# A pairwise embedding tower: chunk 7 of the second batch tile is gathered instead of looked up, under a batch schedule of its own

## The chip, the core and the metric

The kernel runs on one core of one Trainium2 chip. The metric is the device time of one execution, in microseconds (us); three runs of the kernel before have a median of 761.44 us (761.08 to 764.19). Engines are named as in the profile: PE is TensorE, DVE is VectorE, ACT is ScalarE, POOL is GpSimd, SP is the engine that issues most DMAs.

## The reference

2048 samples have 39 ids each. Every id picks a row of 32 numbers from its field's table. For all 741 pairs (i, j) of fields a bilinear form of the two rows is taken with a 32 x 32 matrix of that pair; the 741 sums and 16 dense numbers go through a network of three layers.

```python
e = stack([tbl_f[ids[:, f]] for f in range(39)], axis=1)        # 2048 x 39 x 32
p, q = e[:, ROW, :], e[:, COL, :]                                # all 741 pairs i < j
z = einsum('bpc,apc,bpa->bp', p, w, q)                           # w: 32 x 741 x 32
h = concatenate([z, dense_ctx], axis=1)                          # 757 wide
h = maximum(h @ W_top1 + b_top1, 0)                              # 512
h = maximum(h @ W_top2 + b_top2, 0)                              # 256
y = h @ W_top3                                                   # 1
```

All of it is float32. Products with the pair weights and with the looked-up rows are made of split parts (a rounded part and its rest), so nothing of a value is dropped.

## The kernel before

**Tiles, chunks, batches.** The 2048 samples are 4 tiles of 512. The 39 fields are 10 chunks of four fields (chunk 9 has three); a chunk is named (tile, chunk), as (1, 7). In each tile 200 units are worked through: one unit is one field j against one chunk of partners. Two units are a step, four are a batch. A tile has 50 batches; batches are counted through here, so that tile 1 is batches 50 to 99 and batch 54 is the fifth of tile 1.

**A batch.** PE multiplies four times pair weights by a chunk's stacked values (`u_ps`, line 590). DVE multiplies two units at a time by the partners' values (`prod`, line 911); this needs what PE wrote and releases PE's next but one step. PE sums the products of the batch before (`z_ps`, line 614). In tiles 1 to 3 the batch may hold a piece of the previous tile's network (`m_ps`, line 627, two matmuls of 128x512; called a piece). Where several units of a batch are summed in the same quarter of PE's columns, that sum takes longer.

**How a chunk gets its rows.** Either POOL gathers them: one indirect DMA for each field and each 128 samples, 16 for a chunk (line 419), which land in `e_rows`, and PE turns them around into `t_ps` (`turn`, line 525, four matmuls at line 534). Or, for chunks of small tables (`HOT_TABLES`), they are looked up: DVE compares the ids with row numbers (`one_hot`, line 899), and PE multiplies the result by the table, held in SBUF in three bf16 parts (`look_up`, line 540, matmuls at line 553). A chunk has 10 such slices; slices 0 to 7 have all four fields and 12 matmuls, the last two only the fields of larger tables. Chunks 1, 7 and 8 are looked up in every tile, chunk 2 in tile 0 alone. Three `one_hot` buffers are in turn (`OS = 3`).

After that ACT copies `t_ps` twice (lines 717 and 722), DVE makes the rest (`split_chunk`, line 865), SP stores both to DRAM (`store_parts`) and loads them back in another layout (`stack_chunk`, line 477) into one of four `e4` slots; the first unit of the chunk waits for that load. The first five chunks of tile 0 (`MADE`) are laid out by PE and ACT instead (`make_half`, `take_half`).

**What sets the order.** The tables `FIRST_TILE` and `OTHER_TILES` give, for each chunk: its number, whether it is of the next tile, the batch in which it is turned, and the batches in which its slices are looked up. In a batch PE does its units, a network piece if there is one, the sum of the batch before, then turns, then slices. DVE does two multiplies, then the split of a chunk that was completed in the batch before, then the one-hots of the next batch, then in tile 0 a part of the pair weights' rest (`weights_low`). `spread_mlp` puts the network's 34 pieces into batches with little else. Everything is in order on each engine, with semaphores between.

**Gathers.** POOL issues the gathers in the order of the chunks. The first 96, all of tile 0, wait for the landing of the gather three before (`WINDOW = 3`, line 416). From number 96 on (counted from 0) a gather waits only for a multiply: `s_mul` must reach 45 + (n - 96) * 100 // 108, so 108 gathers are spread over 100 steps (line 418). Number 96 is the first gather of (1, 2). A chunk's gathers also wait until the chunk four places before it has been turned.

Of the kernel before, what the change touches and what calls it, by code (L numbers as in the profile page):

```python
# [10 lines left out]
NT = B // NB  # L11
# [19 lines left out]

def hot(c):

    return c[1] in HOT_TABLES and (c[1] != 2 or c[0] == 0)


def gathered(c):
# [53 lines left out]
def place_sums():  # L91
# [4 lines left out]
    for g, gi, j in UNITS:  # L96
# [9 lines left out]
        if room > n:  # L106
# [12 lines left out]

PACED_FROM, PACE_LEAD = 96, 52  # L120
GATHERS_PER_TILE = 108

E4_SLOT = {0: 0, 1: 2, 2: 3, 3: 1, 7: 2, 8: 3, 4: 0, 5: 1, 6: 0, 9: 1}
OS = 3
# [7 lines left out]
PREPS_FIRST = 2  # L132
PREPS = {max(4 * k - 11, 2 * k - 3 if k < 4 else 6): k for k in range(PREPS_FIRST, len(PREP_UNITS))}

PREP_LOADS = {max(2 if k == 3 else 4, 4 * k - 15, k + 1 if k > 4 else 0): k for k in range(3, len(PREP_UNITS))}

BEGIN = (1, 0)
FIRST_TILE = ((2, 0, 0, (0, 0, 0, 1, 1, 1, 1, 1)), (7, 0, None, (1, 1, 1, 1, 1, 2, 2, 2, 2, 2)), (3, 0, 3, ()), (4, 0, 7, ()),  # L140
# [3 lines left out]
OTHER_TILES = ((8, 0, None, (0, 1, 1, 2, 3, 4, 4, 5, 6, 6)), (4, 0, 7, ()),  # L144
# [12 lines left out]


def chunks_of_tile(t):
    return [x for x in (OTHER_TILES if t else FIRST_TILE) if t + x[1] < NT]  # L160


ORDER = [(0, g) for g in BEGIN] + [(t + nxt, g) for t in range(NT) for g, nxt, turn, slices in chunks_of_tile(t)]
# [81 lines left out]
NI = len(ITEM)  # L245


def spread_mlp(last):

    work = {}  # L250
    for b in range(3, 39 if last else 48):
        slices = sum(list(x[3]).count(b) for x in OTHER_TILES if not (last and x[1]))
        work[b] = 3 * slices + (3 if any(x[2] == b for x in OTHER_TILES) else 0)
    taken = []
    for n in range(len(MLP)):
        b = min(work, key=lambda b: (work[b], b))
        work[b] += 4
        taken.append(b)
    return sorted(taken)


MLP_AT = {last: spread_mlp(last) for last in (False, True)}


def mlp_pieces(batch, last):
    return [piece for piece, b in zip(MLP, MLP_AT[last]) if b == batch]


def ends_tile(tile):
# [11 lines left out]
def tower(nc, tables, ids, hot_ids, hot_rows, dense, w, w1, b1, w2, b2, w3, sel_in, ident_in, y):  # L281
# [4 lines left out]
    with ExitStack() as ctx:  # L286
# [115 lines left out]
        @block.gpsimd  # L402
        def _(pool):
            pool.wait_ge(s_idx, 16)
            issued = 0
            for c in GATHERED:
                t, g = c
                r = GPOS[c] % ER
                if GPOS[c] >= ER:
                    pool.wait_ge(s_tp, GPOS[c] - ER + 1)  # L410
                for q in gathered(c):
                    f = C * g + q
                    for n in range(TPG):
                        if GPOS[c] > 1 and issued < PACED_FROM:
                            before = issued - WINDOW
                            pool.wait_ge(s_rows[GPOS[GATHERS[before]] % ER][before % WINDOW], landed(before))
                        if issued >= PACED_FROM:
                            pool.wait_ge(s_mul, PACED_FROM - PACE_LEAD + 1 + (issued - PACED_FROM) * NS // GATHERS_PER_TILE)
                        pool.indirect_dma_start(  # L419
                            e_rows[:, r, n, D * q:D * q + D], None, tables[f],  # L420
                            bass.IndirectOffsetOnAxis(ap=idx[:, t, f * TPG + n:f * TPG + n + 1], axis=0),
                        ).then_inc(s_rows[r][issued % WINDOW], 16)
                        issued += 1
# [92 lines left out]
        def _(pe):  # L516
# [162 lines left out]
            for t in range(NT):  # L679
                for b in range(NBAT):  # L680
                    for x in range(SPB):
                        interact(t, SPB * b + x)
                    if t:
                        for piece in mlp_pieces(b, t == NT - 1):
                            mlp_piece(t - 1, *piece)
                    if b:
                        reduce(t, b - 1)
                    elif t:
                        reduce(t - 1, NBAT - 1)
                    for c in TURNS.get(NBAT * t + b, ()):  # L690
                        turn(c)
                    for c, k in TAKES.get(NBAT * t + b, ()):
                        look_up(c, k)
                    if t == 0:
                        for c, half in MADE_IN.get(b, ()):
                            make_half(c, half)
                    if t == NT - 1:
                        for m, k in EARLY.get(b, ()):
                            early_piece(t, m, k)
# [3 lines left out]
        def _(act):  # L703
# [121 lines left out]
            for t in range(NT):  # L825
                for b in range(NBAT):
                    if t:
                        for layer, m, k in mlp_pieces(b, t == NT - 1):
                            if k == LAYER_INPUTS[layer] - 1:
                                take_mlp(t - 1, layer, m, m_ps[:, :])  # L830
                    for tile in range(NZ):
                        done = ends_tile(tile) // UPB + 1
                        if done == b:
                            take_z(t, tile)
                        elif t and done == NBAT and b == 0:
                            take_z(t - 1, tile)
                    for c in COMPLETE.get(NBAT * t + b, ()):
                        take_chunk(c)
                    if t == 0:
                        for c, half in MADE_IN.get(b, ()):  # L840
                            take_half(c, half)
                        if b == LAST_TABLE_BATCH:
                            table_high(HOT_CHUNKS[-1])
                        if b == LAST_TABLE_BATCH + 2:
                            table_middle(HOT_CHUNKS[-1])
                        if b - 1 in PREPS:
                            weights_rest(PREPS[b - 1])
                        if b in PREPS:
                            weights_high(PREPS[b])
                        if b in PREP_LOADS:  # L850
                            load_weights(PREP_LOADS[b])
# [7 lines left out]
        def _(dve):  # L859
# [81 lines left out]
            for t in range(NT):  # L941
                for b in range(NBAT):
# [7 lines left out]
                    if t == 0:  # L950
                        if b == LAST_TABLE_BATCH + 1:
                            table_rest(HOT_CHUNKS[-1])
                        if b == LAST_TABLE_BATCH + 3:
                            table_low(HOT_CHUNKS[-1])
                        for c in COMPLETE.get(b, ()):
                            if c in MADE:
                                split_chunk(c)
                    for c, k in TAKES.get(NBAT * t + b + 1, ()):
                        one_hot_slice(c, k)
                    if t == 0 and b in PREPS:  # L960
                        weights_low(PREPS[b])

# [58 lines left out]
```

## Time and profile before

| | |
|---|---|
| three runs, median (lowest to highest) | 761.44 us (761.08 to 764.19) |
| the profiled execution: its own time | 762.68 us |
| its span in the trace | 760.8 us |
| mean granted clock of PE, share of full speed | 0.978 |
| PE busy | 711.1 us (93%) |
| DVE busy | 610.1 us (80%) |
| POOL busy | 411.7 us (54%) |
| ACT busy | 104.5 us (14%) |
| first multiply of tiles 0, 1, 2 and 3 starts at | 40.21, 236.07, 403.67, 572.26 us |

The busy shares are means over stages with different limits. The last line says where the time goes: tile 0 takes 196 us from its first multiply, tiles 1 and 2 take 168 and 169, tile 3 and the end of the network the last 189.

### The profile page before, as it was taken

How to read it: one execution, taken by the hardware profiler on the slowest of the kernel's cores; microseconds unless marked ns; L12 is line 12 of the kernel's file. 1: busy time of each engine (PE TensorE's matmuls, PEld its weight loads, DVE VectorE, ACT ScalarE, POOL GpSimd, SP SyncE). 2: the span in 40 equal slices, each digit the busy share in tenths (PEclk: the TensorE clock that was granted, in tenths of full speed). 3: DMA queues.
4: the chain of work that ended last, by engine and by line, in shares of the span. 5: the costliest groups of instructions: out<-in, count | busy, mean ns of one | idle time of the engine just before them, and what ended most of it. 6: DMA issues, size and time to landing. Idle time of an engine off the chain costs nothing.

```text
span 760.8 us, 10920 instructions
## 1 busy us (share of the span) xinstructions
PE 711.1 (93%) x4202; PEld 285.7 (38%) x4202; DVE 610.1 (80%) x773; ACT 104.5 (14%) x186; POOL 411.7 (54%) x424
## 2 busy tenths in 40 slices
PE   0778888798999999999999999999999999999998
PEld 0233233333334444443434444444334434343343
DVE  3675798899989997998879987998879877788640
ACT  3413301111110100110110101011010101011002
POOL 5777546577776565667656555667655566000000
PEclk9787999999999999999999999999999999999999
DMA  7633987869868382739675472747656373553100
GB/s 205 192 115 87 321 314 235 312 217 307 288 212 289 112 264 75 243 72 307 179 243 184 143 259 64 234 117 243 226 185 233 100 253 88 167 174 105 69 0 0
DMA packets 72271, 141.40 MB, mean 186 GB/s; under 512 B 13829, under 2 KB 23704, under 8 KB 72092
## 3 DMA queue, kind: packets, MB, share of 16 engines
q1 hardware_dynamic: 48796, 116.86, 44.4%
q0 software_dynamic: 13440, 6.91, 6.6%
q10 hardware_dynamic: 9984, 16.94, 6.3%
q8 instruction: 33, 0.54, 0.3%
q14 instruction: 18, 0.15, 0.1%
HBM read 109.66 MB, written 31.00 MB: 185 GB/s over the span
## 4 chain that ended last, share of the span: by engine, by line
PE 81%; DVE 8%; issue 4%; DMA 3%; POOL 2%; ACT 1%; ACTq 0%; SPq 0%; DVEq 0%
PE z_ps L614 26%; PE u_ps L590 26%; PE t_ps L553 10%; PE m_ps L627 8%; DVE prod L911 5%; PE m_ps L629 3%; POOL e_rows L419 2%; DVE one_hot L899 2%; PE t_ps L534 2%; PE u_ps L649 1%; DMA e<-scratch 1%; PE u_ps L658 1%; PE m_ps L631 1%; PE t_ps L641 1%; PE m_ps L641 1%
## 5 line engine op out<-in xcount | busy, mean ns | idle before, releaser
L911 DVE TENSOR_TENSOR prod<-u_ps,eT 128x1024 f32<-128x1024 f32 x400 | 469.6, 1216 | 93.6 <-PE u_ps L590 92.7
L419 POOL DMA_INDIRECT e_rows<-in_tbl_dram,idx x420 | 411.5, 980 | 234.9 <-DVE prod L911 109.5
L590 PE MATMUL u_ps<-e,w 128*128 128x512 f32 x800 | 254.9, 433 | 17.8 <-DVE prod L911 12.9
L614 PE MATMUL z_ps<-prod,sel 128*32 128x512 f32 x1600 | 263.0, 613 | 0.0
L590 PEld LDWEIGHTS u_ps<-e,w 128*128 128x128 f32 x800 | 133.7, 190 | 159.8 <-DVE prod L911 75.8
L553 PE MATMUL t_ps<-one_hot,tb 125*32 125x512 bf16 x1344 | 134.1, 394 | 10.2 <-DVE one_hot L899 8.7
L899 DVE TENSOR_SCALAR one_hot<-hot_idx,row 125x512 bf16<-125x512 f16 (+2 forms) x296 | 108.2, 421 | 13.7 <-PE t_ps L553 11.9
L614 PEld LDWEIGHTS z_ps<-prod,sel 128*32 128x32 f32 x1600 | 43.6, 108 | 137.4 <-issue 111.1
L553 PEld LDWEIGHTS t_ps<-one_hot,tb 125*32 125x32 bf16 x1344 | 48.8, 98 | 91.5 <-issue 59.4
L627 PE MATMUL m_ps<-zT,w1s 128*128 128x512 f32 x144 | 73.5, 592 | 0.0
L717 ACT CAST parts<-t_ps 128x512 fp32r<-128x512 f32 (+1 forms) x40 | 23.5, 587 | 216.1 <-PE t_ps L553 125.1
L781 ACT COPY zT<-z_ps 128x512 f32<-128x512 f32 x24 | 14.1, 587 | 202.0 <-PE z_ps L614 202.0
L865 DVE TENSOR_TENSOR parts<-eT,parts 128x512 fp32r<-128x512 f32 (+1 forms) x40 | 27.2, 680 | 3.8 <-ACT eT L722 3.8
L627 PEld LDWEIGHTS m_ps<-zT,w1s 128*128 128x128 f32 x144 | 27.1, 188 | 6.3
L788 ACT ACTIVATE h<-m_ps,b1s 128x512 f32<-128x512 f32 x13 | 9.0, 689 | 138.4 <-PE m_ps L627 137.1
L629 PE MATMUL m_ps<-h,w2s 128*128 128x512 f32 x48 | 24.5, 592 | 0.0
L722 ACT COPY eT<-t_ps 128x512 f32<-128x512 f32 (+1 forms) x40 | 23.7, 591 | 0.0
L534 PEld LDWEIGHTS t_ps<-ident,e_rows 128*128 128x128 f32 (+2 forms) x112 | 12.2, 143 | 26.3 <-issue 22.9
L534 PE MATMUL t_ps<-ident,e_rows 128*128 128x128 f32 (+2 forms) x112 | 19.3, 298 | 2.6 <-DMA e_rows<-in_tbl_dram,idx 2.6
L872 DVE TENSOR_TENSOR h<-h 128x512 fp32r<-128x512 f32 (+1 forms) x13 | 8.6, 665 | 3.5 <-ACT h L748 3.5
L748 ACT CAST h<-h 128x512 fp32r<-128x512 f32 (+1 forms) x13 | 7.9, 608 | 19.0 <-DMA h<-in_w_dram 10.2
L629 PEld LDWEIGHTS m_ps<-h,w2s 128*128 128x128 f32 x48 | 9.0, 188 | 2.1
(52 smaller groups left out, 124.1 us busy)
## 6 DMA issues: line engine op xcount, KB each, us to landing
w<-w_rows SPq DMA_DIRECT2D x100, 512.0 KB
e<-scratch SPq DMA_DIRECT2D x62, 512.0 KB, 5.8
scratch<-parts SPq DMA_DIRECT2D x62, 256.0 KB
w_rows<-h ACTq DMA_DIRECT2D x48, 256.0 KB
e_rows<-in_tbl_dram,idx POOLq DMA_INDIRECT x420
hot_idx<-hot SPq DMA_DIRECT2D x12, 512.0 KB
h<-in_w_dram ACTq DMA_DIRECT2D x12, 256.0 KB, 4.8
e<-scratch SPq DMA_DIRECT2D x8, 384.0 KB
```

The lines of the kernel that those rows point to most:

```text
L419: pool.indirect_dma_start(e_rows[:, r, n, D * q:D * q + D], None, tables[f], bass.IndirectOffsetOnAxis(ap=idx[:, t, f * TPG + n:f * TPG + ...
L534: last = nc.tensor.transpose(t_ps[0:hi, b * P:b * P + P], rows, ident[:, :])
L553: last = nc.tensor.matmul(t_ps[D * q:D * q + D, :], tb[0:HP, part, col:col + D], one_hot[0:HP, n % OS, here * NB:(here + 1) * NB], start=k ...
L590: last = nc.tensor.matmul(u_ps[:, s % 2, place, :], w4[:, p % WR, (u % PW) * P:(u % PW + 1) * P], e4[:, E4_SLOT[g], j - C * g, :], start=T ...
L614: last = nc.tensor.matmul(z_ps[D * quad:D * quad + D, z % 2, :], sel[:, D - 1 - row:2 * D - 1 - row], prod[:, (NS * t + n) % PR, place, :] ...
L627: last = nc.tensor.matmul(m_ps[:, :], w1s[:, k, m * P:m * P + P], zT[:, t % 2, k, :], start=k == 0, stop=stop)
L629: last = nc.tensor.matmul(m_ps[:, :], w2s[:, k, m * P:m * P + P], h1[:, k, :], start=k == 0, stop=stop)
L717: nc.scalar.copy(parts[0:rows, n % 2, 0, :], t_ps[0:rows, :]).then_inc(s_eh, 1)
L722: nc.scalar.copy(eT[0:rows, e_slot(t, g), :], t_ps[0:rows, :]).then_inc(s_et, 1)
L865: nc.vector.tensor_tensor(parts[0:rows, n % 2, 1, :], eT[0:rows, e_slot(t, g), :], parts[0:rows, n % 2, 0, :].bitcast(F32), ALU.subtract). ...
L899: last = nc.vector.tensor_scalar(one_hot[0:HP, n % OS, i * NB:(i + run) * NB], hot_idx[0:HP, LPOS[c] % 2, x * NB:(x + run) * NB], (row10 i ...
L911: nc.vector.tensor_tensor(prod[:, s % PR, :, :], u_ps[:, s % 2, :, :], e, ALU.mult).then_inc(s_mul, 1)
```

## The change

Chunk (1, 7) is no longer looked up but gathered. Tile 1 gets a table of its own, `SECOND_TILE`; tiles 2 and 3 keep `OTHER_TILES`. The pace of the gathers is 124 for 100 steps over the first 124 paced ones and 108 after that. In tile 0 three of the ten slices of (0, 7) are in batch 1 where five were, and seven in batch 2; the split of (0, 2) stands behind the one-hots of batch 0 instead of behind the multiplies of batch 1; the load of the pair weights' part 3 is issued in batch 1 instead of batch 2. (1, 2) is turned in batch 39 instead of 40. The network pieces are spread by the tile's own table.

```diff
 def hot(c):
-    return c[1] in HOT_TABLES and (c[1] != 2 or c[0] == 0)
+    return c[1] in HOT_TABLES and (c[1] != 2 or c[0] == 0) and c != (1, 7)
@@
+MORE_GATHERS = 16
+def gather_step(n):
+    more = n - PACED_FROM
+    second = GATHERS_PER_TILE + MORE_GATHERS
+    return PACED_FROM - PACE_LEAD + 1 + (more * NS // second if more < second else NS + (more - second) * NS // GATHERS_PER_TILE)
@@
-PREP_LOADS = {max(2 if k == 3 else 4, 4 * k - 15, k + 1 if k > 4 else 0): k for k in range(3, len(PREP_UNITS))}
+PREP_LOADS = {max(1 if k == 3 else 4, 4 * k - 15, k + 1 if k > 4 else 0): k for k in range(3, len(PREP_UNITS))}
@@
-FIRST_TILE = ((2, 0, 0, (0, 0, 0, 1, 1, 1, 1, 1)), (7, 0, None, (1, 1, 1, 1, 1, 2, 2, 2, 2, 2)), (3, 0, 3, ()), (4, 0, 7, ()),
+FIRST_TILE = ((2, 0, 0, (0, 0, 0, 1, 1, 1, 1, 1)), (7, 0, None, (1, 1, 1, 2, 2, 2, 2, 2, 2, 2)), (3, 0, 3, ()), (4, 0, 7, ()),
...
-              (7, 1, None, (32, 32, 33, 33, 34, 35, 35, 36, 37, 38)), (2, 1, 40, ()), (0, 1, 43, ()), (3, 1, 48, ()))
+              (2, 1, 39, ()), (0, 1, 43, ()), (3, 1, 48, ()))
+SECOND_TILE = ((7, 0, 4, ()), (4, 0, 8, ()), (8, 0, None, (9, 9, 10, 10, 11, 11, 12, 12, 13, 14)), (5, 0, 17, ()),
+               (1, 1, None, (18, 19, 20, 20, 21, 22, 23, 24, 24, 25)), (6, 0, 26, ()),
+               (7, 1, None, (27, 28, 29, 30, 31, 32, 33, 33, 34, 35)), (9, 0, 36, ()),
+               (2, 1, 39, ()), (0, 1, 43, ()), (3, 1, 49, ()))
@@
-                            pool.wait_ge(s_mul, PACED_FROM - PACE_LEAD + 1 + (issued - PACED_FROM) * NS // GATHERS_PER_TILE)
+                            pool.wait_ge(s_mul, gather_step(issued))
@@
                         for c in COMPLETE.get(b, ()):
-                            if c in MADE:
+                            if c in MADE and c != (0, 2):
                                 split_chunk(c)
                     for c, k in TAKES.get(NBAT * t + b + 1, ()):
                         one_hot_slice(c, k)
+                    if t == 0 and b == 0:
+                        split_chunk((0, 2))
```

What this makes of the order is shown at two places. On PE, tile 1 from its third batch (batch 52) on. `u_ps` rows open a batch, `t_ps<-one_hot` rows are slices (12 matmuls each), `t_ps<-ident,e_rows` is the turn of a gathered chunk, `m_ps` a network piece. Before, batches 53 to 57, which end with the turn of (1, 4):

```order
L590 MATMUL u_ps<-e,w 128x512 x4
L627 MATMUL m_ps<-zT,w1s 128x512
L614 MATMUL z_ps<-prod,sel 32x512 x4
L553 MATMUL t_ps<-one_hot,tb 32x512 x12
L590 MATMUL u_ps<-e,w 128x512 x4
L614 MATMUL z_ps<-prod,sel 32x512 x4
L553 MATMUL t_ps<-one_hot,tb 32x512 x24
...
L590 MATMUL u_ps<-e,w 128x512 x4
L627 MATMUL m_ps<-zT,w1s 128x512
L614 MATMUL z_ps<-prod,sel 32x512 x4
L534 MATMUL t_ps<-ident,e_rows 128x128 x4
```

And now batches 54, 58 and 59, with the turns of (1, 7) and (1, 4) and the first two slices of (1, 8):

```order
L604 MATMUL u_ps<-e,w 128x512 x4
L641 MATMUL m_ps<-zT,w1s 128x512
L628 MATMUL z_ps<-prod,sel 32x512 x4
L548 MATMUL t_ps<-ident,e_rows 128x128 x4
...
L604 MATMUL u_ps<-e,w 128x512 x4
L641 MATMUL m_ps<-zT,w1s 128x512
L628 MATMUL z_ps<-prod,sel 32x512 x4
L548 MATMUL t_ps<-ident,e_rows 128x128 x4
L604 MATMUL u_ps<-e,w 128x512 x4
L628 MATMUL z_ps<-prod,sel 32x512 x4
L567 MATMUL t_ps<-one_hot,tb 32x512 x24
```

The slices of (1, 8), which stood in batches 50 to 56, stand in batches 59 to 64, two to a batch at first, and the turn of (1, 4) has moved from batch 57 to 58. On DVE the same place, batches 57 to 59 (a slice of chunk 8 or 1 is three one-hot instructions, 125x512, 125x512 and 125x1024). Before:

```order
L911 TENSOR_TENSOR prod<-u_ps,eT 128x1024 x4
L865 TENSOR_TENSOR parts<-eT,parts 128x512
L899 TENSOR_SCALAR one_hot<-hot_idx,row 125x512
L899 TENSOR_SCALAR one_hot<-hot_idx,row 125x1024
L899 TENSOR_SCALAR one_hot<-hot_idx,row 125x512
L911 TENSOR_TENSOR prod<-u_ps,eT 128x1024 x2
```

Now, batches 58 and 59:

```order
L925 TENSOR_TENSOR prod<-u_ps,eT 128x1024 x6
L913 TENSOR_SCALAR one_hot<-hot_idx,row 125x512 x2
L913 TENSOR_SCALAR one_hot<-hot_idx,row 125x1024
L913 TENSOR_SCALAR one_hot<-hot_idx,row 125x512 x2
L913 TENSOR_SCALAR one_hot<-hot_idx,row 125x1024
L925 TENSOR_TENSOR prod<-u_ps,eT 128x1024 x2
L879 TENSOR_TENSOR parts<-eT,parts 128x512
```

DVE has nothing but multiplies from batch 56 on until the one-hots of batch 59, two slices at once, and the split of (1, 4) comes with the next two slices.

## Rows read from the trace of the kernel before

**Rows 1.** The page's first part: busy time of each engine.
```profile
PE 711.1 (93%) x4202; PEld 285.7 (38%) x4202; DVE 610.1 (80%) x773; ACT 104.5 (14%) x186; POOL 411.7 (54%) x424
```

**Rows 2.** Length; PE, PEld, DVE, ACT, POOL busy; clock; DMA share; GB/s, by stretch of batches.
```profile
176.85:204.11 27.26, 25.73 (x203) 10.15 (x204) 26.85 (x38) 3.08 (x7) 21.17 (x21) 1.00 0.97 330
204.11:236.07 31.96, 30.64 (x157) 11.33 (x158) 29.00 (x29) 4.28 (x8) 23.29 (x25) 1.00 0.72 231
236.07:265.55 29.48, 29.48 (x223) 12.73 (x216) 27.67 (x46) 2.50 (x5) 17.32 (x18) 1.00 0.52 170
265.55:291.38 25.83, 25.83 (x181) 10.83 (x181) 23.71 (x38) 1.51 (x3) 14.87 (x15) 1.00 0.68 224
291.38:360.14 68.76, 68.76 (x411) 28.62 (x410) 58.95 (x66) 8.13 (x14) 43.38 (x46) 1.00 0.58 179
360.14:403.67 43.53, 43.21 (x204) 16.87 (x202) 35.51 (x35) 6.39 (x12) 28.32 (x31) 1.00 0.62 196
```

**Rows 3.** Timeline of PE: a turn, a slice, a piece, a long sum.
```profile
263.96 0.66 PE L534 MATMUL t_ps<-ident,e_rows 128*128 128x128 f32 x4
264.37 1.17 PE L590 MATMUL u_ps<-e,w 128*128 128x512 f32 x4
...
293.47 0.83 PE L553 MATMUL t_ps<-one_hot,tb 125*32 125x512 bf16 x12
294.24 1.21 PE L590 MATMUL u_ps<-e,w 128*128 128x512 f32 x4
...
347.45 1.20 PE L590 MATMUL u_ps<-e,w 128*128 128x512 f32 x4
348.49 1.02 PE L627 MATMUL m_ps<-zT,w1s 128*128 128x512 f32 x2
349.44 1.07 PE L614 MATMUL z_ps<-prod,sel 128*32 128x512 f32 x8
350.43 1.20 PE L590 MATMUL u_ps<-e,w 128*128 128x512 f32 x4
...
618.44 1.90 PE L614 MATMUL z_ps<-prod,sel 128*32 128x512 f32 x8
```

**Rows 4.** Timeline of DVE: multiplies, a split, two slices each of chunks 7 and 8.
```profile
191.25 1.66 DVE L899 TENSOR_SCALAR one_hot<-hot_idx,row 125x1536 bf16<-125x1536 f16 x4
...
403.67 2.34 DVE L911 TENSOR_TENSOR prod<-u_ps,eT 128x1024 f32<-128x1024 f32 x2
405.93 0.67 DVE L865 TENSOR_TENSOR parts<-eT,parts 128x512 fp32r<-128x512 f32 x1
406.53 1.96 DVE L899 TENSOR_SCALAR one_hot<-hot_idx,row 125x512 bf16<-125x512 f16 x6
408.41 2.34 DVE L911 TENSOR_TENSOR prod<-u_ps,eT 128x1024 f32<-128x1024 f32 x2
```

**Rows 5.** POOL's gathers: timeline at number 96, then counts by stretch.
```profile
156.42 0.94 POOL L419 DMA_INDIRECT e_rows<-in_tbl_dram,idx  x1 [0.30 <-issue]
157.67 0.95 POOL L419 DMA_INDIRECT e_rows<-in_tbl_dram,idx  x1 [0.30 <-issue]
...
77.00:157.60 80.60, 43.79 (x44) 0.94 0.86 295
157.60:218.80 61.20, 46.81 (x48) 1.00 0.80 261
```

**Rows 6.** The chain that ended last, at the start: a gather's landing.
```profile
25.94 4.57 DMA e_rows<-in_tbl_dram,idx
```

**Rows 7.** Two stretches of different PE clock, and PE in the second.
```profile
50.60:57.40 6.80, 3.85 (x62) 1.53 (x64) 6.16 (x12) 0.78 (x2) 5.28 (x6) 1.00 0.11 16
57.40:67.60 10.20, 8.73 (x41) 2.79 (x41) 2.18 (x6) 2.67 (x5) 7.76 (x9) 0.50 0.22 64
...
115.40:122.20 6.80, 4.93 (x28) 1.79 (x23) 4.73 (x6) 1.59 (x3) 4.97 (x7) 1.00 0.48 133
122.20:125.70 3.50, 3.50 (x12) 1.09 (x13) 2.65 (x3) 0.62 (x1) 2.87 (x3) 0.51 0.98 308
```

**Rows 8.** The line of the stack loads (L477).
```profile
DMA to landing us min/median/max: 3.8/5.8/8.7
```

More of the change, by code:

```diff
@@ L159, in chunks_of_tile @@
 def chunks_of_tile(t):
-    return [x for x in (OTHER_TILES if t else FIRST_TILE) if t + x[1] < NT]
+    return [x for x in (FIRST_TILE, SECOND_TILE, OTHER_TILES, OTHER_TILES)[t] if t + x[1] < NT]
 ORDER = [(0, g) for g in BEGIN] + [(t + nxt, g) for t in range(NT) for g, nxt, turn, slices in chunks_of_tile(t)]
@@ L245, with spread_mlp @@
 NI = len(ITEM)
-def spread_mlp(last):
+def spread_mlp(t):
     work = {}
-    for b in range(3, 39 if last else 48):
-        slices = sum(list(x[3]).count(b) for x in OTHER_TILES if not (last and x[1]))
-        work[b] = 3 * slices + (3 if any(x[2] == b for x in OTHER_TILES) else 0)
+    for b in range(3, 39 if t == NT - 1 else 48):
+        slices = sum(list(x[3]).count(b) for x in chunks_of_tile(t))
+        work[b] = 3 * slices + (3 if any(x[2] == b for x in chunks_of_tile(t)) else 0)
     taken = []
@@ L259, in spread_mlp, with mlp_pieces @@
     return sorted(taken)
-MLP_AT = {last: spread_mlp(last) for last in (False, True)}
-def mlp_pieces(batch, last):
-    return [piece for piece, b in zip(MLP, MLP_AT[last]) if b == batch]
+MLP_AT = {t: spread_mlp(t) for t in range(1, NT)}
+def mlp_pieces(batch, t):
+    return [piece for piece, b in zip(MLP, MLP_AT[t]) if b == batch]
 def ends_tile(tile):
@@ L683, in _ @@
                     if t:
-                        for piece in mlp_pieces(b, t == NT - 1):
+                        for piece in mlp_pieces(b, t):
                             mlp_piece(t - 1, *piece)
@@ L827, in _ @@
                     if t:
-                        for layer, m, k in mlp_pieces(b, t == NT - 1):
+                        for layer, m, k in mlp_pieces(b, t):
                             if k == LAYER_INPUTS[layer] - 1:
```

## The prediction

> **What bounds the kernel now.** The page's first part comes first: PE is busy 93% of the span and DVE 80% [rows 1]. PE is the likely bound, but DVE is near enough to bound stretches of its own, so the next view is busy time by stretch of batches, cut at the first multiply of a batch [rows 2]. In batches 31 to 38, where the slices of (1, 7) lie, DVE is busy 26.85 of 27.26 us and PE 25.73: DVE binds. In batches 50 to 57, with the slices of (1, 8), PE is busy 29.48 of 29.48 us and DVE 27.67: they are about level. In batches 58 to 85 PE has no gap at all (25.83 of 25.83 and 68.76 of 68.76 us), and DVE has about 10 us of room in the second of these. So work taken out of batches 31 to 57 is worth its time, and slices put into batches 65 to 85 cost theirs on PE.
>
> Prices of single things come from the timelines. On PE the four products of a batch take 348.49 - 347.45 = 1.04 us, a network piece 0.95, the sum 0.99 [rows 3]. A slice shows as 294.24 - 293.47 = 0.77 us, but the sum ahead of it is then about 0.12 shorter, so I take 0.65; a turn takes 0.41, and a long sum 0.84 more than a plain one (1.90 against 1.07) [rows 3]. On DVE the two multiplies of a batch take 405.93 - 403.67 = 2.26 us, a split 0.60, a slice of chunk 8 or 1 0.94 (1.88 for two), a slice of chunk 7 0.79 (1.66 for two, less 0.08 that lie beside the next instruction) [rows 4]. For the last two slices of a chunk I take an estimate of a third of that (0.7 for chunk 8, which keeps three fields), for `weights_low` that of a split. A batch costs what the dearer engine needs. By this rule batches 31 to 38, 39 to 49, 50 to 57, 58 to 64, 65 to 85 and 86 to 99 come to 27.2, 29.4, 28.9, 26.4, 67.9 and 42.1 us; measured are 27.26, 31.96, 29.48, 25.83, 68.76 and 43.53 [rows 2]. It is short by up to 8%, but I use it for differences only.
>
> The last view is POOL's. Its gathers are issued no closer than 1.25 us (156.42, 157.67) [rows 5]. The 44 gathers between 77 and 157.6 us take 1.83 us each, since each waits for the landing of the third before. Number 96, the first that is paced by the multiplies, goes out at 157.67 us. Its pace would have let it go after step 45, in batch 22, about 7 us sooner. From there POOL runs nearly without a gap: 48 gathers in 61.2 us [rows 5]. So POOL is late there, though its busy share is 54% [rows 1].
>
> **The change, part by part.**
>
> *Start.* The split of (0, 2) comes some 3 us sooner, but two slices of (0, 7) then stand behind `make_half` instead of in a time when PE waited. The part of the order on PE is a swap of about equal sizes: -3 to +3 us, and I take 0. It is on no path that sets the end, as the gathers show below: they are bound up to number 95 by their landings and not by steps.
>
> *Batches 31 to 49.* Ten slices of (1, 7) go: 8 full ones of 0.65 on PE and 0.79 on DVE, two small ones. Batches 31 to 38 fall from 27.2 to 20.1 us by the rule (DVE: eight pairs of multiplies 18.1, a split and two parts of weights 1.8, by itself 19.9): -7.1. In batches 39 to 49 the split of (1, 7) and the first one-hot of (1, 8) go from DVE: 29.4 to 28.4, -1.0.
>
> *Batches 50 to 57.* Ten slices of (1, 8) leave; two network pieces come. PE: 8 x 2.03 + 5 x 0.95 + 0.41 = 21.4; by batch 22.1 instead of 28.9: -6.8.
>
> So batch 58 would begin at 265.55 - 14.9 = 250.65 us. That multiply starts when PE has done its first pair of products, some 0.65 us of the batch's 1.04 + 0.95 + 0.99 = 2.98. PE would so reach the turn of (1, 4), which now stands in batch 58, 2.3 us later, at 253.0.
>
> *The gathers.* The changed pace asks for 124 in 100 steps, and the steps themselves have become shorter: 31 to 57 had 3.3 us a batch and would have 2.7, so 1.35 us a step and 1.09 us for a gather. POOL can do no better than 1.25. The last gather of (1, 4) was number 159 and is now number 175, since the 16 of (1, 7) are ahead of it. Counted from number 96 at 157.67 it goes out no sooner than 157.67 + 79 x 1.25 = 256.4 us. It must land: the one landing that the chain shows took 4.57 us [rows 6], three in flight at 1.83 us each are 5.5 us, and a back-to-back run with three in flight could not be kept up if it took over 3.75. Between 0.94 (its own instruction) and 5.5 I take 3.5, as POOL runs back to back here too: 259.9 us. PE waits there 7 us. Turn and first product pair (0.41 and about 0.65) put the first multiply of batch 59 at 261.0 instead of 269.34: -8.3 us is left of the -14.9, and the extra cost of batch 58's own DVE work (4.1 against 3.8) is hidden in the wait. Whatever the start gains or loses within 7 us vanishes here as well. Behind the waiting turn in PE's order are the products of batch 59 and the slices of (1, 8), so DVE waits with it. The turn of (1, 7) itself, in batch 54, meets a last gather at 157.67 + 63 x 1.25 + 3.5 = 239.9 us and is reached at about 240: no wait, or 1 to 2 us that only shorten the later one. Its stack load must be there by batch 59. Split in batch 55, store and load of at most 8.7 us [rows 8] end before 260, so the wait for (1, 4) covers it; without that wait it could cost 1 us.
>
> *Batches 59 to 99.* The slices are closer together now. Batches 59 to 64: DVE has eight slices of (1, 8) and a split in four batches, 24.4 instead of 22.6: +1.8. Batches 65 to 85: 7 full slices more (7 x 0.65) and two pieces more (2 x 0.95) are 6.5 on PE, 73.4 instead of 66.9; by batch 74.6 against 67.9: +6.7. Nothing hides them, since PE had no gap there. Batches 86 to 99: +0.4, a split. Together +8.9. The order of tiles 2 and 3 is the same and the gathers are level again by then (number 219 could go out at 157.67 + 123 x 1.25 = 311.4, about when its step is done).
>
> *PE's clock.* Twice in tile 0 the granted clock fell to half (1.2 of 2.4 GHz) after a stretch with waits: after 50.6 to 57.4, with PE busy 3.85 of 6.80 us, for 10.2 us, and after 115.4 to 122.2, busy 4.93 of 6.80, for 3.5 us [rows 7]. A wait of 7 us leaves PE emptier than either. A batch of products, sum and two slices takes PE 3.3 us and at half clock at worst 6.6, against DVE's 4.1, so 2.5 us of each 6.6 are lost: 1.3 us for a stretch of 3.5 us, 3.9 for one of 10.2. I take +1.5, nearer to the short one, as the fall may come within the wait.
>
> The Trainium skill says of this, in "TensorE: Matmul & The Clock Gate", section "HAM oscillation — how this bites in real kernels", that a wait for a DMA between bursts of matmuls lets the array fall back to half rate, and the next burst pays for it. The trace agrees [rows 7]. By that rule the change costs something at the very place where it frees PE; if it didn't hold, the sum would be 1.5 us less.
>
> *Sum.* -8.3 + 8.9 + 1.5 = +2.1 us. Against the profiled execution's own 762.68 us that is 764.8; it ran 1.24 above the median of the runs, so for the median I say 761.44 + 2.1 = 763.5 us.
>
> **Rivals.**
>
> *The gathers keep up.* If the last of (1, 4) lands by 253.0, nothing waits: -14.9 + 0.3 + 8.9 = -5.7, so 755.7 us. For it: the 7 us by which number 96 is late hang on landings in a crowded stretch (DMA busy share 0.86), and these could go otherwise. Against it: even from 150 us on, 79 gathers of 1.25 and a landing end at 252.3, so all of the lateness would have to go.
>
> *The gathers are later still.* On the other side: issue at 61.2 / 48 = 1.275 us and a landing of 5.5 put the first multiply of batch 59 at 157.67 + 100.7 + 5.5 + 1.1 = 265.0, -4.3 instead of -8.3, and a longer wait makes the half clock last 10.2 us, +3.9: in all +8.5, 769.9 us. It decides as soon as the landing is after 259.9; each us from there counts whole. For it: stretches 31 to 49 move their DMA bytes in less time, at 330 GB/s already [rows 2]. Against it: part of the 61.2 us was waiting for the pace, which now asks sooner.
>
> *The rule by batches is too dear.* If half of the +8.9 in batches 59 to 99 is hidden (DVE runs ahead into light batches), the time is 759 us. Against it: PE's total of added work alone is 6.5 in batches 65 to 85.
>
> **How the numbers follow.** The forecast, wait at (1, 4) and net about +2, has a chance of 0.5 with a range of 759.5 to 767.5; the gathers keeping up 0.2; later still 0.18; cheaper batches 0.12. A change of under 0.5%, 3.8 us, can't be told from none. Above 765.2 lie a good third of the forecast's chance and all of the later-still case: 0.34. Below 757.6 lie the keeping-up case and a little of the others: 0.24. Same: 0.42. The range of 8 in 10 reaches from the one rival to the other: 754.5 to 770.
>
> **What would show it.** In the profile after: an idle PE of 5 to 9 us in front of the turn (its line L548) once, near 253 to 260 us, released by the gathers' landing; POOL's gathers at 1.25 us apart from about 157 to 280 us without a wait for DVE; number 96 still near 157; first multiplies of batches 50 and 58 near 228 and 251, of tile 2 near 405; PE's clock at half for 3 to 10 us behind the wait; the stretch of batches 65 to 85 near 75 us. It is wrong if PE doesn't wait at that turn, if tile 2 begins before 400 us, or if batches 31 to 57 aren't some 15 us shorter.

## Result, and the profile after

The changed kernel takes 764.96 us (median of 20 runs, 762.86 to 768.77) where the kernel before took 762.0 on the same chips (20 runs, 760.77 to 764.19). The ratio is 1.0047, 95% interval 1.0035 to 1.0059: slower by about 3.6 us, which is just short of the 0.5% taken as no change. The forecast was 763.5 us with a range of 754.5 to 770. On some chips used for the experiments the kernel before itself took about 888 us, and in the profiles taken there (of other kernels) the first multiply starts at 91 to 103 us instead of 40; what ran there is kept apart below, as inconclusive.

The profiled execution took 764.9 us by itself, with a span of 763.0 (before: 762.68 and 760.8). The first part of its page, which answers to [rows 1]:

```profile
PE 706.3 (93%) x4104; PEld 283.9 (37%) x4104; DVE 603.8 (79%) x755; ACT 104.4 (14%) x186; POOL 426.0 (56%) x440
```

PE has 4.8 us less work, DVE 6.3 us less, POOL 14.3 us more, and yet the span is 2.2 us longer. The same stretches of batches as in [rows 2], 31 to 38, 39 to 49, 50 to 57, 58 to 64, 65 to 85 and 86 to 99, with the same columns:

```profile
172.19:192.82 20.63, 19.12 (x100) 6.47 (x100) 19.81 (x21) 2.58 (x5) 15.75 (x17) 1.00 1.01 357
192.82:227.11 34.29, 29.59 (x146) 11.06 (x146) 27.34 (x26) 3.82 (x7) 26.06 (x28) 1.00 0.68 224
227.11:252.49 25.38, 25.38 (x119) 10.35 (x118) 19.44 (x19) 1.66 (x3) 19.29 (x21) 1.00 0.56 184
252.49:286.94 34.45, 28.03 (x209) 11.94 (x208) 26.14 (x44) 2.94 (x6) 26.22 (x28) 0.90 0.44 140
286.94:362.43 75.49, 75.49 (x499) 32.08 (x498) 66.53 (x90) 8.14 (x15) 50.29 (x53) 1.00 0.57 179
362.43:405.94 43.51, 43.19 (x204) 16.88 (x202) 35.93 (x36) 6.86 (x13) 28.06 (x30) 1.00 0.69 220
```

Lengths against before: -6.6, +2.3, -4.1, +8.6, +6.7 and 0.0 us. At batch 31 the changed kernel was 4.7 us ahead (172.19 against 176.85). Of these, 2.3 were there at the first multiply already (37.95 against 40.21), ahead of every edit; in the four later profiles below it starts at 39.55 to 41.40, with or without the edits of the start, so this part is the chance of one execution. At batch 58 it was 13.1 us ahead, at batch 59 6.6 (262.77 against 269.34), and at batch 86 2.3 behind. Tile 2 begins at 405.94 instead of 403.67, and that difference stays to the end. PE is idle for 4.7 us of the second stretch (1.3 before) and for 6.4 of the fourth, which had no gap; most of the gain goes there. PE's timeline there, the idle time and its releaser in brackets:

```profile
260.79 1.09 PE L548 MATMUL t_ps<-ident,e_rows 128*128 128x128 f32 x4 [6.03 <-DMA e_rows<-in_tbl_dram,idx]
261.53 2.06 PE L604 MATMUL u_ps<-e,w 128*128 128x512 f32 x4
263.51 1.94 PE L628 MATMUL z_ps<-prod,sel 128*32 128x512 f32 x8
...
266.88 1.20 PE L604 MATMUL u_ps<-e,w 128*128 128x512 f32 x4
```

The turn of (1, 4) waits 6.03 us for a gather. The chain that ended last goes through this wait and shows what made the gather late (start, length, what):

```profile
255.78 1.02 POOL e_rows L433
256.80 0.30 issue
257.10 0.95 POOL e_rows L433
258.05 0.30 issue
258.36 2.34 DMA e_rows<-in_tbl_dram,idx
260.70 0.09 issue
260.79 1.09 PE t_ps L548 x4
```

The gather at 258.36 is number 175, the last of (1, 4). POOL came to it with one gather behind the other, 1.25 us apart. The counts of gathers by stretch, up to number 95 and from 96 to 174, answer to [rows 5]:

```profile
77.00:157.10 80.10, 46.59 (x47) 0.93 0.82 279
157.10:258.30 101.20, 77.10 (x79) 1.00 0.72 242
```

### The profile page after: what moved, and what is told of

Its sections match the earlier page's. It is cut to its first block, busy times and chain, and to the rows that moved or that the text cites. A ratio compares the mean times of both kernels' runs of the same rounds, so it can differ in the third digit from the quotient of the medians.

```text
span 763.0 us, 10722 instructions
## 1 busy us (share of the span) xinstructions
PE 706.3 (93%) x4104; PEld 283.9 (37%) x4104; DVE 603.8 (79%) x755; ACT 104.4 (14%) x186; POOL 426.0 (56%) x440
## 4 chain that ended last, share of the span: by engine, by line
PE 78%; DVE 10%; issue 5%; DMA 3%; ACT 2%; POOL 1%; ACTq 1%; SPq 0%; DVEq 0%
PE z_ps L628 25%; PE u_ps L604 24%; PE t_ps L567 9%; PE m_ps L641 8%; DVE prod L925 6%; DVE one_hot L913 3%; PE m_ps L643 3%; PE t_ps L548 2%; PE u_ps L663 1%; POOL e_rows L433 1%; DMA e<-scratch 1%; DMA e_rows<-in_tbl_dram,idx 1%; PE u_ps L672 1%; PE m_ps L645 1%; DMA hot_idx<-hot 1%
## 5 line engine op out<-in xcount | busy, mean ns | idle before, releaser
L433 POOL DMA_INDIRECT e_rows<-in_tbl_dram,idx x436 | 425.8, 977 | 222.8 <-DVE prod L925 94.1
L604 PE MATMUL u_ps<-e,w 128*128 128x512 f32 x800 | 256.4, 435 | 17.8 <-DVE prod L925 12.9
L567 PE MATMUL t_ps<-one_hot,tb 125*32 125x512 bf16 x1242 | 119.5, 396 | 10.6 <-DVE one_hot L913 9.1
L913 DVE TENSOR_SCALAR one_hot<-hot_idx,row 125x512 bf16<-125x512 f16 (+2 forms) x278 | 101.1, 422 | 11.0 <-PE t_ps L567 8.8
L567 PEld LDWEIGHTS t_ps<-one_hot,tb 125*32 125x32 bf16 x1242 | 44.7, 99 | 85.3 <-issue 57.7
```

The source lines that it names most:

```text
L433: pool.indirect_dma_start(e_rows[:, r, n, D * q:D * q + D], None, tables[f], bass.IndirectOffsetOnAxis(ap=idx[:, t, f * TPG + n:f * TPG + ...
L567: last = nc.tensor.matmul(t_ps[D * q:D * q + D, :], tb[0:HP, part, col:col + D], one_hot[0:HP, n % OS, here * NB:(here + 1) * NB], start=k ...
L604: last = nc.tensor.matmul(u_ps[:, s % 2, place, :], w4[:, p % WR, (u % PW) * P:(u % PW + 1) * P], e4[:, E4_SLOT[g], j - C * g, :], start=T ...
L913: last = nc.vector.tensor_scalar(one_hot[0:HP, n % OS, i * NB:(i + run) * NB], hot_idx[0:HP, LPOS[c] % 2, x * NB:(x + run) * NB], (row10 i ...
```

## The experiments

Each kernel was timed against the kernel before on its own chip.

**Four gathers in flight.** The changed kernel with one number different:

```diff
-WINDOW = 3
+WINDOW = 4
```

> The changed kernel with four gathers in flight instead of three for the first 96, again, since the chip of the first try ran the kernel before in 888 us and not in 762, from its first 100 us on. Theory of the late gathers: number 96 goes out near its step, at 145 to 148 us instead of 157.2, the waits of PE at the turns of (1, 3) and (1, 4) shrink to under 1 us each, the half clock behind the second goes, and tile 2 begins about 10 us sooner: 753 to 756 us, a ratio to before of about 0.990. Rival, the closer slices: the waits are small beside what batches 59 to 99 cost, and 1 or 2 us come back at most: 763 to 765 us.

Measured: 757.58 us (755.84 to 758.58, 6 runs), ratio to before 0.9934 (0.9917 to 0.9951), span 756.7. The same kernel was faster than before by 0.66% where three in flight made it slower by 0.47%. POOL at number 96, and PE at the turn of (1, 4):

```profile
144.83 0.94 POOL L433 DMA_INDIRECT e_rows<-in_tbl_dram,idx  x1 [0.30 <-issue]
149.33 0.94 POOL L433 DMA_INDIRECT e_rows<-in_tbl_dram,idx  x1 [3.55 <-DVE prod L925]
150.58 1.02 POOL L433 DMA_INDIRECT e_rows<-in_tbl_dram,idx  x1 [0.30 <-issue]
```

```profile
253.44 1.06 PE L628 MATMUL z_ps<-prod,sel 128*32 128x512 f32 x8
255.45 0.63 PE L548 MATMUL t_ps<-ident,e_rows 128*128 128x128 f32 x4 [0.94 <-DMA e_rows<-in_tbl_dram,idx]
255.83 1.18 PE L604 MATMUL u_ps<-e,w 128*128 128x512 f32 x4
```

Number 96 goes out at 149.33 instead of 157.17, and the engine is now idle for 3.55 us ahead of it, until the multiply that its pace asks for, where with three in flight it was late by the landings. From there to number 175 the rate is the same (79 gathers in 100.3 us, 1.27 each), so the last one goes out at 249.62 instead of 258.36, and the turn waits 0.94 us. Its landing took longer, 5.58 us instead of 2.34:

```profile
249.62 5.58 DMA e_rows<-in_tbl_dram,idx
255.20 0.25 issue
255.45 0.63 PE t_ps L548 x4
```

Batch 58 began in both at the same time, 252.22 and 252.49, and batch 59 at 256.57 and 262.77. The 6.2 us between them are there to the end (756.68 and 763.04). So the wait is the cause of the missing gain, and the lateness of number 96 is the cause of the wait. The start of this execution was 3.5 us slower than that of the three in flight (90.06 at batch 7 against 86.56), so the gain didn't come from there. It was made up before batch 58 by a second wait for gathers that is gone as well, in batch 48. Lengths of the batches against before, in us:

| batches | forecast | three in flight | four in flight |
|---|---|---|---|
| 31 to 38 | -7.1 | -6.6 | -6.6 |
| 39 to 49 | -1.0 | +2.3 | -1.0 |
| 50 to 57 | -6.8 | -4.1 | -4.1 |
| 58 | +6.6, the wait | +6.5 | +0.6 |
| 59 to 99 | +8.9, and 1.5 for the clock | +8.8 | +8.6 |

The two kernels differ in the stretches with the two waits and nearly nowhere else. By the table they are 9.4 us apart, by the ratios 8.6. The ratio of about 0.990 that was expected would have been 11, more than the two waits and the clock had cost.

**The start alone.** The kernel before with the three edits of the start (the one of the split stands in two places):

```diff
-PREP_LOADS = {max(2 if k == 3 else 4, ...
+PREP_LOADS = {max(1 if k == 3 else 4, ...
-FIRST_TILE = (..., (7, 0, None, (1, 1, 1, 1, 1, 2, 2, 2, 2, 2)), ...
+FIRST_TILE = (..., (7, 0, None, (1, 1, 1, 2, 2, 2, 2, 2, 2, 2)), ...
-                            if c in MADE:
+                            if c in MADE and c != (0, 2):
+                    if t == 0 and b == 0:
+                        split_chunk((0, 2))
```

> The kernel before with the three edits of the start alone, again on another chip. Theory of the late gathers: the 4.5 us that batch 7 of the changed kernel is ahead are real, and here no turn waits for a gather, so they reach the end: about 757.5 us, ratio 0.994. Rival, the start is absorbed here too, by gathers that go out no sooner: under 1 us, ratio above 0.9985.

Measured: 759.75 us (757.22 to 761.89, 8 runs), ratio 0.9969 (0.9953 to 0.9985). The start is worth 2.4 us where nothing takes it back, between the 4.5 expected and the rival's less than 1. From the first multiply to that of batch 7 it takes 47.1 us in this kernel and 50.8 before. In the changed kernel it takes 48.6, so 2.2 of the 4.5 us that it was ahead at batch 7 are the edits', and the rest is the chance head start.

**Without the start.** The changed kernel with the same three edits taken back.

> The changed kernel without the three edits of the start, again on another chip. Theory of the late gathers: the wait in front of the turn of (1, 4) ends when its last gather lands, near 261 us, whatever the start does, so losing 4.5 us at the start costs nothing: the same as the changed kernel within 1 us, ratio to before 1.003 to 1.006. Rival, the start's gain is in the time of the changed kernel: 4.5 us slower than it, ratio 1.010.

Measured: 767.46 us (765.79 to 767.88), ratio 1.0064 (1.0048 to 1.008). Batch 7 begins at 91.25 instead of 86.56. Of these 4.7 us, 2.6 lie ahead of the first multiply (40.59 against 37.95), where the kernels don't differ. Some 3 are left at the end (span 766.0 against 763.0) in this one execution; by the ratios it is 0.17%, 1.3 us, and the intervals overlap. PE's waits for gathers between 200 and 300 us (total, times, longest):

```profile
PE t_ps L548 <- DMA e_rows<-in_tbl_dram,idx: 6.8, 2, 4.5
```

In the changed kernel they are 9.3 us:

```profile
PE t_ps L548 <- DMA e_rows<-in_tbl_dram,idx: 9.3, 2, 6.0
```

A later PE waits less, by 2.5 us in the two waits together. The difference is still 4.4 us at batch 58 and 2.9 at batch 59: the last wait absorbs 1.5, and not all, since number 96 went out later too, at 161.24. Whether the start brought that about isn't shown.

**The slices of (1, 8) and (2, 1) sooner.** This puts lookups into the time in which PE outran the gathers, and the turn of (1, 4) two batches later:

```diff
-SECOND_TILE = ((7, 0, 4, ()), (4, 0, 8, ()), (8, 0, None, (9, 9, 10, 10, 11, 11, 12, 12, 13, 14)), (5, 0, 17, ()),
-               (1, 1, None, (18, 19, 20, 20, 21, 22, 23, 24, 24, 25)), (6, 0, 26, ()),
-               (7, 1, None, (27, 28, 29, 30, 31, 32, 33, 33, 34, 35)), (9, 0, 36, ()),
+SECOND_TILE = ((7, 0, 4, ()), (8, 0, None, (5, 5, 6, 6, 7, 7, 8, 8, 9, 9)), (4, 0, 10, ()),
+               (1, 1, None, (11, 12, 12, 13, 14, 15, 16, 17, 17, 18)), (5, 0, 19, ()),
+               (7, 1, None, (20, 21, 22, 23, 24, 25, 26, 26, 27, 27)), (6, 0, 28, ()), (9, 0, 36, ()),
```

> The kernel of g1 once more, for a chip on which the kernel before takes 762 us: the slices of (1, 8) in batches 55 to 59, ahead of the turn of (1, 4) in batch 60, three gathers in flight. Theory of the late gathers: no wait of over 1 us at that turn and no half clock there, the wait in batch 48 stays; tile 2 begins 8 to 10 us sooner than in the changed kernel, near 397 us, and the time is 754 to 757 us, ratio 0.990 to 0.993. Rival, the closer slices: nothing is gained beyond 2 us: ratio above 1.001.

Measured: 764.55 us (762.07 to 767.18, 12 runs), ratio 1.0032 (1.0017 to 1.0047). A miss: the ratio is the one that the rival named. The wait at the turn of (1, 4) is gone, as intended (batch 58 takes 3.59 us instead of 10.28), but another one is there. PE in batch 64:

```profile
279.56 0.96 PE L604 MATMUL u_ps<-e,w 128*128 128x512 f32 x3
282.93 0.79 PE L604 MATMUL u_ps<-e,w 128*128 128x512 f32 x1 [2.40 <-DMA e<-scratch]
```

And the chain that leads to it:

```profile
270.71 0.69 DVE parts L879
271.42 5.98 DMA scratch<-parts
277.46 0.58 SPq L491
278.08 4.80 DMA e<-scratch
282.93 0.79 PE u_ps L604
```

The split of (1, 4), its store and its stack load take 12.2 us from 270.71, and the first product that needs the chunk comes sooner than that: it has stayed in batch 64, while the turn moved from batch 58 to 60. The clock fell to half again as well, from 282.5 to 285.9. Batch 64 took 7.71 us where it takes 3.63 in the changed kernel, 4.1 of the 7.2 that the wait at the turn and its half clock had cost. The 8 to 10 us expected were more than there was to win. Moved in this way, the lookups shifted the lateness by one step, from the gather to the store and load behind it.

**Inconclusive.** Three more kernels ran only on chips where the kernel before takes 888 us: the kernel before with four in flight, this last kernel with four in flight, and the start alone with four in flight.

> The kernel before with four gathers in flight instead of three for the first 96. Theory of the late gathers: no turn of the kernel before waits for a gather in tile 1, so sooner gathers are worth nothing: ratio 0.998 to 1.001. Rival, more gathers in flight in tile 0 is itself a gain or a loss (DMAs of the pair weights delayed, or a turn that did wait): off by over 1.5 us.

> The kernel of g1 with four gathers in flight for the first 96. Theory of the late gathers: only the wait in batch 48 is left to win, 2 to 3 us less than g1: 752 to 755 us, ratio 0.987 to 0.990. Rival, gathers crowd the start: slower than g1 by 1 us or more.

> The kernel before with the three edits of the start and four gathers in flight: the fourth gather where chunk (1, 7) is still looked up. Theory of the late gathers: no turn of this kernel waits for a gather in tile 1, so it is the same as with the start's edits alone, ratio 0.995 to 0.998, and gathering (1, 7) is worth the 2 to 3 us between this and the changed kernel with four in flight (0.9934). Rival, four in flight are a gain by themselves: 0.993 or less, and gathering (1, 7) is worth nothing.

Measured there: 893.91 us (ratio to the kernel before there 1.0049, 1.0012 to 1.0086), 909.3 (1.0207, 1.0172 to 1.0243) and 892.49 (1.0095, 1.0038 to 1.0152). The four experiments above were first run on such chips as well, the last of them twice. Their expectations, in the order of the text:

> The changed kernel with four gathers in flight instead of three for the first 96. Theory of the late gathers: number 96 goes out near its step, at 145 to 148 us instead of 157.2, the waits of PE at the turns of (1, 3) and (1, 4) (5.97 us for batch 48, 10.3 for batch 58) shrink to under 1 us each, the half clock behind the second goes, and tile 2 begins about 10 us sooner: 753 to 756 us, a ratio to before of about 0.990. Rival, the closer slices: the waits are small beside what batches 59 to 99 cost, and nothing but 1 or 2 us comes back: 763 to 765 us.

> The kernel before with the three edits of the start alone: three slices of (0, 7) in batch 1, the split of (0, 2) before the multiplies of batch 1, the load of pair weights' part 3 in batch 1. Theory of the late gathers: the 4.5 us that batch 7 of the changed kernel is ahead are real, and here no turn waits for a gather, so they reach the end: about 757.5 us, ratio 0.994. Rival, the start is absorbed here too, by gathers that go out no sooner: under 1 us, ratio above 0.9985.

> The changed kernel without the three edits of the start. Theory of the late gathers: the wait in front of the turn of (1, 4) ends when its last gather lands, near 261 us, whatever the start does, so losing 4.5 us at the start costs nothing: the same as the changed kernel within 1 us, ratio to before 1.003 to 1.006. Rival, the start's gain is in the time of the changed kernel: 4.5 us slower than it, ratio 1.010.

> The changed kernel with three gathers in flight as it has, but with the slices of (1, 8) in batches 55 to 59, ahead of the turn of (1, 4), which moves from batch 58 to 60; the later slices of tile 1 move up a little. The gathers go out as late as in the changed kernel. Theory of the late gathers (what the change loses is PE's wait for them, and work put ahead of the turn fills it): the turn is reached after 260.7 us, no wait of over 1 us and no half clock there, the wait in batch 48 stays; tile 2 begins 8 to 10 us sooner, near 397 us, and the time is 754 to 757 us, ratio 0.990 to 0.993. Rival, the closer slices: by dearer engine the batches of tile 1 add up as in the changed kernel, 168.3 us against 167.8, so nothing is gained beyond 2 us: ratio above 1.001.

> The kernel of g1 again, since the chip of that run ran the kernel before in 889 us: the changed kernel with three gathers in flight, but with the slices of (1, 8) in batches 55 to 59, ahead of the turn of (1, 4), which moves from batch 58 to 60. Theory of the late gathers (what the change loses is PE's wait for them, and work put ahead of the turn fills it): no wait of over 1 us at that turn and no half clock there, the wait in batch 48 stays; tile 2 begins 8 to 10 us sooner, near 397 us, and the time is 754 to 757 us, ratio 0.990 to 0.993. Rival, the closer slices: by dearer engine the batches of tile 1 add up as in the changed kernel, 168.3 us against 167.8, so nothing is gained beyond 2 us: ratio above 1.001.

There the changed kernel with four in flight, which is the fastest elsewhere, came to 908.13 us (1.0215, 1.0156 to 1.0275), the start alone to 886.45 (before 888.23, no interval), the changed kernel without it to 907.82 (1.018, 1.0127 to 1.0234), and the two runs with the sooner slices to 900.24 (1.011, 1.0064 to 1.0155) and 904.79 (1.0164, 1.0104 to 1.0224). The kernels rank otherwise there, so nothing about the other chips follows. The traces show one reason why a fourth gather in flight could win nothing: with three, number 95 was out long before the pace let number 96 go. POOL in the changed kernel without the start:

```profile
173.96 1.25 POOL L433 DMA_INDIRECT e_rows<-in_tbl_dram,idx  x1 [1.42 <-DMA e_rows<-in_tbl_dram,idx]
228.49 0.94 POOL L433 DMA_INDIRECT e_rows<-in_tbl_dram,idx  x1 [53.28 <-DVE prod L925]
```

The lateness that the experiments were about was not there, and PE waited for no gather in tile 1. Why the changed kernel loses 1 to 2% on these chips is not shown. Whether four gathers in flight would help the kernel before too, with (1, 7) looked up, is open.

## Why the prediction was right, and where it was off

**The mechanism holds.** The forecast named the turn of (1, 4) in batch 58, a wait of 7 us for the last gather, number 96 near 157, and POOL back to back from there. Measured are 6.03 us, 157.17, and 79 gathers in 101.2 us. Step by step: the last gather was due at 256.4 at 1.25 us each and went at 258.36 (1.28 each); the landing was taken at 3.5 us and took 2.34; the turn was due at 259.9 and began at 260.79. Two errors of about 2 and 1.2 us, in opposite directions. One reason given for the 3.5 doesn't hold: that gathers back to back with three in flight must land within 3.75 us. From number 96 on the kernel waits for no landing, and with four in flight number 175 took 5.58 us in just such a run. That the landing took 2.34 us here was luck. The rival in which the gathers keep up is shown by the run with four in flight: without the wait the change gives 757.58 us. That this is near the 755.7 worked out for it is in part luck too, since 2.4 us of its gain are the start, which the prediction had at nothing; from batch 31 to 99 the trace has -2.5 us where that rival had -5.7.

A reader should see one trap in this chain. It enters POOL's run at 252.04, behind a multiply that ended at 251.87, as if the pace had bound there:

```profile
250.65 1.23 DVE prod L925
251.87 0.17 issue
252.04 0.94 POOL e_rows L433
252.98 0.30 issue
```

But POOL's gap ahead of that gather is the usual 0.30 us, and with four in flight the same gather (number 170, five before 175) went out at 249.62 - 5 x 1.25 = 243.4 behind the same steps. Its pace asks for multiply 45 + 74 * 100 // 124 = 104, the last of batch 51, which begins at 230.39 us. The multiply only ended within a gap that is always there.

**Start.** It was priced at 0 (-3 to +3 us) and said to be on no path that sets the end. Alone it is worth 2.4 us. The split of (0, 2) was to come 3 us sooner; counted from the first multiply it comes 5.3 sooner (10.9 us behind it instead of 16.2). The wait of 2.12 us of `make_half` for the split of (0, 2) is gone, since the split now stands ahead of batch 1's multiplies instead of behind them:

```profile
48.83 0.68 DVE L879 TENSOR_TENSOR parts<-eT,parts 128x512 fp32r<-128x512 f32 x1
49.43 2.34 DVE L925 TENSOR_TENSOR prod<-u_ps,eT 128x1024 f32<-128x1024 f32 x2
```

Before, it began at 56.40. In the changed kernel the statement that the wait swallows the start is mostly right and not wholly: number 96 isn't a fixed time. It went out at 157.67, 157.17, 158.10, 161.24 and 158.96 in the five profiles with three in flight, and doesn't follow the start (batch 7 at 91.04 and 91.25 goes with 157.67 and 161.24, at 86.56 and 86.63 with 157.17 and 158.10). What sets it within these 4 us is open.

**Batches 31 to 38**: -7.1 forecast, -6.6 measured. **39 to 49**: -1.0 forecast, +2.3 measured. Batch 49 gave its 1.1 us, but batch 48 took 5.97 instead of 2.65, with a wait that the prediction didn't have, at the turn of (1, 3):

```profile
223.11 0.63 PE L548 MATMUL t_ps<-ident,e_rows 128*128 128x128 f32 x4 [3.28 <-DMA e_rows<-in_tbl_dram,idx]
```

It is the same lateness of POOL, met one chunk sooner. The prediction looked for it at the turns of (1, 7) and (1, 4) alone. With four in flight it is gone too (batch 48: 2.65).

**Batches 50 to 57**: this is the term that was mis-sized, -6.8 forecast and -4.1 measured. The largest part is a price left out. The sums of batches 51, 52 and 55 are long ones, 1.90 us instead of 1.07; in each of them two neighbouring units go to the same quarter of PE's columns:

```profile
230.75 1.90 PE L628 MATMUL z_ps<-prod,sel 128*32 128x512 f32 x8
232.58 1.20 PE L604 MATMUL u_ps<-e,w 128*128 128x512 f32 x4
233.71 1.91 PE L628 MATMUL z_ps<-prod,sel 128*32 128x512 f32 x8
```

The 0.84 stood among the prices [rows 3] and was left out of PE's side of these batches. Batch by batch, the rule gave batches 51 and 52 the 2.26 us of their multiplies and batch 55 2.98; they took 2.97, 2.96 and 3.85, so 0.7, 0.7 and 0.9 too much. Batch 50 took 3.27 instead of 2.26, with the matmuls of the dense numbers (line 612) beside the last sum of tile 0; before, that batch took 4.10 us by DVE's work, and they were hidden. The other four are right to 0.02. That is 3.3 us, less the 0.6 by which the rule was short before (28.9 against 29.48). Before, the long sums were there as well, but matmuls of slices lay between their parts. Batch 51 of the kernel before:

```profile
239.27 1.04 PE L614 MATMUL z_ps<-prod,sel 128*32 128x512 f32 x4
239.74 0.39 PE L553 MATMUL t_ps<-one_hot,tb 125*32 125x512 bf16 x1
239.74 1.01 PE L614 MATMUL z_ps<-prod,sel 128*32 128x512 f32 x3
240.17 0.60 PE L553 MATMUL t_ps<-one_hot,tb 125*32 125x512 bf16 x5
240.58 0.59 PE L614 MATMUL z_ps<-prod,sel 128*32 128x512 f32 x1
```

So the slices that left had in part used time that a long sum leaves free, and taking them out gave back less than their price. How much of the 2.7 us this is was not measured by itself.

**Both errors, 3.3 and 2.7 us, cost the forecast nothing.** By its own signs it was wrong here: batches 31 to 57 were to be some 15 us shorter and are 8.4 (80.3 against 88.7), 11.7 without the wait in batch 48. That batches 50 and 58 nevertheless began near the 228 and 251 named, at 227.11 and 252.49, is luck: the 4.7 us by which the kernel was ahead at batch 31, where the forecast had 0, stood in for the missing ones. But all of this lies ahead of the wait in batch 58, and its end is set by the gathers: with batch 58 reached sooner, PE would only have waited longer. So the gain at batch 59, -8.3 forecast and -6.6 measured, is off only by what the gathers and the clock were off.

**PE's clock.** +1.5 us was taken. The clock stood at half in the second of these three stretches (columns as in [rows 7]), from inside the wait on:

```profile
252.10:258.90 6.80, 2.66 (x14) 0.86 (x12) 4.56 (x8) 0.69 (x1) 5.28 (x6) 1.00 0.57 211
258.90:265.70 6.80, 4.91 (x24) 2.50 (x28) 2.93 (x4) 1.07 (x2) 5.12 (x6) 0.50 0.22 55
265.70:272.50 6.80, 6.80 (x76) 3.03 (x72) 6.72 (x16) 0.59 (x1) 5.13 (x6) 1.00 0.51 156
```

Of these 6.8 us some 2 lie in the wait itself. From the turn to the next multiply it took 262.77 - 260.79 = 1.98 us, against 256.57 - 255.45 = 1.12 at full clock with four in flight, and batches 59 and 60 a further 0.36 us more: 1.2 in all. The rule of the Trainium skill that the prediction weighed ("TensorE: Matmul & The Clock Gate", "HAM oscillation — how this bites in real kernels") holds here: the clock fell in the wait, and the burst behind it paid. With a wait of 0.94 us it did not fall.

**Batches 59 to 99**: +8.9 forecast, 143.17 against 134.33 measured, +8.8. Batches 59 to 64 took 24.17 us (24.4 forecast), 65 to 85 75.49 (near 75). PE has no gap in the latter, so each slice and piece put there costs its full price, and the rival of cheaper batches falls.

The forecast's sum was +2.1; the profiled executions show +2.2, and the ratio of all runs +3.6. The close match is in part luck, with 2.3 us of chance head start in the one profiled execution.

## The version that beats both

The changed kernel with four gathers in flight, 0.9934 (0.9917 to 0.9951), is the fastest. The start alone gives 0.9969 (0.9953 to 0.9985). The two intervals just don't overlap; the 2 to 3 us between them belong to the gathered (1, 7) and the fourth gather together. The trace puts 2.5 us into batches 31 to 99. As the kernel before with four in flight ran only on the chips of 888 us, no time shows how much of this needs the gathered (1, 7).

## What to carry to other kernels

Before work is moved from a busy engine to a queue with a low busy share, count the queue forward from the point where it is last known to be late, at its closest spacing, to the item that is needed; a share of 54% over the span said nothing about a stretch in which POOL had no gap. Then ask what sets that starting point: here it was the number in flight, and one more turned +0.5% into -0.7%. What is gained ahead of such a wait, and what is mis-sized there, is taken by it alike; only what lies behind it adds up.

## What the runs showed of the hardware

Indirect gathers of one kind went out 1.25 us apart at the closest, 0.94 us each and 0.30 between. Up to number 95, where each had to wait for the landing three or four before, numbers 52 to 95 went out 1.72 us apart with three in flight (81.98 to 155.93) and 1.56 with four (77.56 to 144.83). It was not every gather that waited: with three in flight, ten in a row went out 1.25 to 1.30 us apart (106.89 to 118.19). Landings differed much from one gather to the next: between 200 and 262 us, where neither kernel holds a gather back for a landing, those that the traces time took 2.3 to 5.5 us in the one and 2.3 to 6.2 in the other. And the half clock cost much less than half its length, 1.2 of 6.8 us; 1.9 of the 6.8 lay in the wait.
